# Attention over a patched on-chip pool: blocks kept in SBUF, 16 pairs instead of 32 sequences

## The reference

```
x = x + einsum('bct,bcd->bdt', x, W0[cond])                     # layer 0: a 32 x 32 mix per sequence
x = x + x @ W1.T + scaled low-rank adapter (rank 16 of 8)        # layer 1
q, k, v = x @ Wq.T, x @ Wk.T, x @ Wv.T                           # layer 2: 8 query heads, 4 key heads of 32
q, k = rope(rms(q)), rope(rms(k))                                # positions kv_lens .. kv_lens + 31
blk = block_tables[b, pos // 16]
k_blocks[blk, :, pos % 16] = k;  v_blocks[blk, :, pos % 16] = v  # the new rows are written into the pool first
scores = q . all keys of the sequence's table, masked to the last 128 positions; softmax; . v;  @ Wo.T
x = x + attention;   x = x + x @ W3[id] + b3[id]                 # layer 3: one of 16 experts per sequence
```

## Time and profile before

| | |
|---|---|
| runs | 164.04, 165.34, 165.74 us |
| profiled execution, first to last instruction | 177.7 us |
| mean granted TensorE clock in it | 0.932 |
| PE / DVE / ACT / POOL busy | 136.0 / 98.0 / 95.6 / 82.3 us |
| first scores | 63.9 us |

### The profile page before, as it was taken

The page is one execution under the profiler, slowest core; times in us unless marked ns, Lnnn a source line. Parts: engine busy times, 40 slices in busy tenths (PEclk is TensorE's granted clock), DMA queues, the critical chain, the costliest instruction groups (busy, mean ns, idle before and its releaser), DMA issues.

```text
span 177.7 us, 4258 instructions
## 1 busy us (share of the span) xinstructions
PE 136.0 (77%) x1414; PEld 93.1 (52%) x1414; DVE 98.0 (55%) x376; ACT 95.6 (54%) x288; POOL 82.3 (46%) x121
## 2 busy tenths in 40 slices
PE   0022989999899368969669659769959979999972
PEld 0012975999698233434235335357636556757741
DVE  0878803798346202795659356326746477975120
ACT  0007479694455724844999705446565666771200
POOL 3477500078377772185543876415677531421000
PEclk9999999999999978988999985856996999999999
DMA  4975990823793377012197776362256463655650
GB/s 89 331 174 178 404 411 24 365 107 118 295 376 101 96 253 330 0 65 59 36 391 272 216 204 191 122 220 73 89 195 191 114 211 115 185 156 161 204 178 31
DMA packets 21727, 32.57 MB, mean 183 GB/s; under 512 B 5162, under 2 KB 18730, under 8 KB 20682
## 3 DMA queue, kind: packets, MB, share of 16 engines
q1 hardware_dynamic: 15536, 19.76, 33.3%
q0 software_dynamic: 2960, 11.67, 18.9%
q10 hardware_dynamic: 3210, 0.87, 2.2%
HBM read 23.91 MB, written 8.39 MB: 182 GB/s over the span
## 4 chain that ended last, share of the span: by engine, by line
PE 67%; ACT 11%; issue 8%; DVE 6%; DMA 5%; another core or an unknown queue 2%; ACTq 0%; DVEq 0%
PE bank L1178 7%; PE bank L1162 7%; PE bank L1208 6%; PE bank L1221 5%; PE bank L1195 4%; PE bank L1066 4%; PE bank L1079 4%; PE bank L1055 4%; DMA kvn<-in_L_cond_weights,cond_i 3%; ACT pr L703 3%; PE bank L1216 3%; PE bank L1004 3%; ACT blkp L587 2%; PE bank L1039 2%; PE bank L1067 2%
## 5 line engine op out<-in xcount | busy, mean ns | idle before, releaser
L703 ACT ACTIVATE pr<-S,nb 128x160 f32<-128x160 f32 x64 | 27.0, 427 | 12.8 <-DVE nb L943 7.4
L943 DVE CUSTOM_DVE_ANT_0 S<-bank,mask 128x160 f32<-128x160 f32 x64 | 18.2, 319 | 17.5 <-PE bank L1162 10.2
L1162 PE MATMUL bank<-KT,QT 32*64 32x160 f32 x256 | 20.9, 341 | 6.2 <-DVE nb L943 3.4
L511 POOL TENSOR_TENSOR prB<-pr,ri 128x64 f32<-128x64 f32 x32 | 9.4, 295 | 29.8 <-DVE ri L928 29.7
L932 DVE TENSOR_SCALAR pr<-pr,ri 128x128 f32<-128x128 f32 x64 | 22.1, 389 | 1.1
L482 POOL DMA_INDIRECT blkp<-kv_rows,rowA x16 | 16.9, 1058 | 7.7 <-DMA kv_rows<-blkp 5.4
L482 POOL DMA_INDIRECT kvA<-kv_rows,rowA x16 | 16.3, 1022 | 6.4 <-issue 3.4
L690 ACT COPY PTA<-bank 128x256 f32<-128x256 f32 x32 | 12.0, 375 | 13.0 <-PE bank L1178 10.2
L1162 PEld LDWEIGHTS bank<-KT,QT 32*64 32x64 f32 x256 | 8.8, 138 | 15.9 <-issue 9.6
L1178 PE MATMUL bank<-cst,pr 128*128 128x128 f32 x64 | 14.0, 304 | 0.5
L703 ACT ACTIVATION_READ_ACCUMULATOR pr<-S,nb 128x1 f32 x64 | 12.5, 195 | 0.0
(11 more groups left out here) (206 smaller groups left out, 313.1 us busy)
## 6 DMA issues: line engine op xcount, KB each, us to landing
We<-in_L_cond_W SPq DMA_DIRECT2D x16, 256.0 KB
kvn<-in_L_cond_W SPq DMA_DIRECT2D x16, 256.0 KB
kv_rows<-blkp SPq DMA_DIRECT2D x1, 2048.0 KB, 6.5
kv_rows<-blk SPq DMA_DIRECT2D x1, 2048.0 KB
kv_rows<-blkp SPq DMA_DIRECT2D x4, 512.0 KB, 4.9
xin<-in_x SPq DMA_DIRECT2D x2, 512.0 KB, 5.6
kv_rows<-kvn SPq DMA_DIRECT2D x2, 512.0 KB, 2.8
be<-in_L_cond_b SPq DMA_DIRECT2D x32, 32.0 KB
```

Of the source, the lines that this page charges most:

```text
L703: act.activation(pr[:, n // B4 % 2, u, n % B4, :], S[:, n % 2, u, :], ACT.Exp, bias=nb[:, n % 4, u:u + 1], scale=-1.0, accum_out=rs[:, n % ...
L943: dve.tensor_tensor_reduce(S[:, n % 2, u, :], bank[2 + (2 * n + u) % 3][:, 0:KEYS], mask[:, n, :], -SCALE, 3e38, ALU.add, ALU.min, nb[:, n ...
L1162: i_ = mm(bank[2 + i % 3][GS * T * k:GS * T * k + GS * T, 0:KEYS], QT[h, g, j, :], KT[h, g % 2, j, :], start=True, stop=True)
```

## The change

Nearly every function is touched. What it does:

- **Blocks.** A unit now holds the 11 blocks of 11, 11 and 10 sequences. All eight raw transfers (the 96 blocks that are written, K and V, and three units of K and V) are of 128 blocks; POOL issues them in one run. The permuted units stay in SBUF (`blkp`), by row in the block.
- **Writes.** The 96 written blocks go to DRAM (`wr_rows`, 1.5 MB), eight indexed stores put the 1,024 new rows there, and three indexed loads copy the finished written blocks over those partitions of `blkp` whose block was written; other indices are out of bounds and skipped. The 40 gathers of rows are gone.
- **Keys** are turned on PE from `blkp` (`turn_k`, 12 calls of 4, L1043), into KT for all 32 sequences. **Values** go out with the unit to DRAM (2 MB, `values_out`) and come back by row (`values_back`, four transfers of 512-byte pieces a unit).
- **Masks.** One strip of 318 distances is squared and compared once, written to DRAM, and read back 32 times at 32 offsets (`load_mask`, 128 pieces of 352 bytes). The 32 distance rows on ACT and the 8 mask instructions on DVE are gone.
- **q** is projected from x2 after layer 1, two products a tile, with no composed Wq; layer 1 and all q norms now come before the loop.
- **Loop** of 16 pairs over 176 columns (before 160): one exponential per sequence and half as before, but one normalising per pair on POOL (L520, 128 x 704), one copy of 512 and one of 256 columns on ACT. On PE the product with V trails the scores by three pairs, before by eight sequences. Tails are turned per pair.
- **Experts** are loaded without the biases (those are eight indexed loads on POOL); DVE adds the identity to each expert's diagonal blocks (L951), which replaces L1216. Sixteen experts have room where units 0 and 2 lay.
- **Start.** PE begins with 12 products of ones whose results nobody reads; W1 is loaded from ACT's queue, most small loads from SP's.

The core of the diff (removed lines are the old functions above; a line of "..." leaves lines out):

```
-            for n in range(B + TAIL):
-                if n + 1 < B:
-                    scores(n + 1)
...
+            for n in range(PAIRS):
+                if n + 1 < PAIRS:
+                    scores(n + 1)
+                for c in KT_STEP.get(n, ()):
+                    turn_k(c)
+                g = group_at(n, PROJECT)
+                if g is not None:
+                    project(g)
+                if n >= TURN:
+                    turn_probs(n - TURN)
+                if n >= PV:
+                    pv(n - PV)
+                if g is not None:
+                    layer3(g)
...
+            def load_mask(b):
+                x = sp.value_load(shift_i[0:1, b:b + 1], min_val=0, max_val=LAST)
+                sp.dma_start(mask[:, b, :], mask_rows[:, bass.ds(x, KEYS)]).then_inc(s_mask, 16)
...
+            for b in range(8):
+                load_mask(b)
+            for kv in range(2):
+                sp.wait_ge(s_perm[NU, kv], 1)
+            sp.dma_start(wr_blocks, blkw[0:NWI, :]).then_inc(s_base, 16)
+            for b in range(8, B):
+                load_mask(b)
...
+            values_out(0)
+            values_back(0)
+            values_out(1)
+            for b in range(4):
+                expert(b)
+            values_back(1)
+            values_out(2)
+            for b in range(4, 8):
+                expert(b)
+            values_back(2)
...
+            pool.wait_ge(s_new, 16 * NT)
+            pool.wait_ge(s_pidx, 1)
+            for u in range(NU):
+                for kv in range(2):
+                    pool.wait_ge(s_perm[u, kv], 1)
+                pool.indirect_dma_start(out=blkp[u][:, :], out_offset=None, in_=wr_blocks,
+                                        in_offset=bass.IndirectOffsetOnAxis(ap=patch_i[:, u:u + 1], axis=0),
+                                        bounds_check=NWI - 1, oob_is_err=False).then_inc(s_patch[u], 16)
...
+            for p in range(PAIRS - 1):
+                pool.wait_ge(s_ri, p + 1)
+                e_ = pr[:, p % 2, :, :].rearrange("p u r -> p (u r)").rearrange("p (i r) -> p i r", i=4)
+                pool.tensor_tensor(e_, e_, ri[:, p % 2, :].unsqueeze(2).broadcast_to([P, 4, KEYS]),
+                                   ALU.mult).then_inc(s_pn, 1)
...
+                    if n == 0:
+                        dve.wait_ge(s_mask, 16 * B)
+                        dve.wait_ge(s_new, 16 * NT)
...
+                    dve.wait_ge(s_we[g % B4], 16 * B4 * (g // B4 + 1))
+                    for kc in range(KC):
+                        w_ = We4(g)[:, :, kc, kc * P:(kc + 1) * P]
+                        tt(w_, w_, ident.unsqueeze(1).broadcast_to([P, B4, P]), ALU.add).then_inc(s_wx, 1)
```

More of the change, by code:

```diff
@@ L380, in _ @@
             for g in range(NT):
[L381 removed]
+                while nxt < B and (nxt - NE) // B4 <= g - 1:
                     expert(nxt)
@@ L544, in distances @@
-            def distances(g):
-                for j in range(B4):
-                    distance(g, j)
+            act.wait_ge(s_kvT, 1)
+            act.copy(WkvT, square(0)).then_inc(s_kvTk, 1)
+            act.wait_ge(s_mixz, 1)
+            act.wait_ge(s_mixt, 1)
+            for h, q in MIX_ACT:
+                dst, src = mix_part(h, q)
+                act.copy(dst, src).then_inc(s_mixA, 1)
+            act.wait_ge(s_w1T, 1)
+            act.copy(W1T, square(0)).then_inc(s_w1Tk, 1)
+            act.wait_ge(s_aT, 1)
@@ L1058, in project_kv @@
-            def project_kv(v, i):
-                pe.wait_ge(s_xas, i + 1)
+            def project_kv(v, i, tiles=(0, 1, 2, 3)):
+                if not v and tiles[0] == 0:
+                    pe.wait_ge(s_xas, i + 1)
+                    pe.wait_ge(s_cmpk, 2)
+                    pe.wait_ge(s_aTk, 2)
                 w = slice(KV * v, KV * v + KV)
-                for t in range(4):
+                for t in tiles:
                     o = bank[1 + 2 * v + i][:, t * KV:t * KV + KV]
@@ new lines, in _ @@
+            mix_down(0)
+            mix_down(1)
+            pe.wait_ge(s_qw, 16)
+            turn_square(7, nat, 1).then_inc(s_qT, 1)
+            pe.wait_ge(s_diag, 4)
+            pe.wait_ge(s_set, 2)
+            pe.wait_ge(s_w1Tk, 1)
+            for u in range(4):
+                n = PU[u] if u < NU else NWI
+                c0 = UCOL[u] if u < NU else FLAT
+                i_ = mm(bank[0][0:NWI, c0:c0 + n], ones[0:n, 0:NWI], diag[0:n, u, 0:n], start=True, stop=True)
+            i_.then_inc(s_brd, 1)
@@ new lines, in _ @@
+            CNT = FLAT + NWI
+            down(0)
+            pe.wait_ge(s_inr, 3)
+            mm(bank[0][0:NWI, CNT:CNT + BLOCK + 1], later[:, :], wr[:, 2, :], start=True, stop=True).then_inc(s_cnt, 1)
+            down(1)
+            pe.wait_ge(s_can, 1)
+            mm(bank[0][0:NWI, CNT + 20:CNT + 21], same[:, :], own[:, 0:1], start=True, stop=True)
+            for u in range(NU):
+                i_ = mm(bank[0][0:PU[u], CNT + 24 + u:CNT + 25 + u], hit[:, UCOL[u]:UCOL[u] + PU[u]], own[:, 0:1], start=True, stop=True)
```

1425 lines of the change are left out of this document (671 added, 754 removed).

## The result

| | before | changed |
|---|---|---|
| runs, median (us) | 165.34 | 154.90 (154.64 to 156.95) |
| profiled execution, span (us) | 177.7 | 153.1 |
| spans of single runs (us) | | 152.9, 153.1, 155.1 |
| mean granted clock | 0.932 | 0.90 |
| PE / DVE / ACT / POOL busy (us) | 136.0 / 98.0 / 95.6 / 82.3 | 117.3 / 88.8 / 85.8 / 62.0 |

The changed kernel takes 0.952 of the time before, 95% interval 0.938 to 0.967. It is faster, by 10 us and not by 24. The forecast of the span, 152, is met within 1.1 us, and every run of the changed kernel is 1.8 us above its own span. The forecast of the run time, 141, is missed by 14.

The account below looks back on a forecast made before the run. PE was taken to bound the loop. First scores at 71, 63.3 of PE's loop, 10 of fill, drain and bubbles, 3.0 of output, 3 for clock, 2 overlooked gave a span of 152 us; as runs 141, range 130 to 157.

Parts of the forecast that it names:

- As runs: Last step: span 152 converted to run time by the old profile's 12.4 us excess, as constant or ratio, giving 141.
- Up to the first scores: Stage before the loop: first scores at 71 us, 7 us later than in the kernel before.
- The covers: POOL's stores, patches and bias gathers, mask loads and values, each costed at nothing as hidden under other work.
- Mask loads: Loads on SP's queue, 1.15 us each, the last 24 ending at 59 us; costed at nothing.
- rival 3: Masks late: DVE's first maximum waits for all 32 loads; at 2.9 us a load, runs 169; chance 0.08.
- Values: Trip through DRAM: a 2 MB unit lands 6.5 us after issue, out at 60, back by 73; costed at nothing.
- The loop's groups: PE's group of four sequences in the loop: 7.33 us against 8.24, eight groups 58.6.
- The remaining allowances: Added to PE's loop work: 10 us for fill, drain and bubbles, 3 for the clock, 2 for what is overlooked.
- A rule against the change: In the loop, DVE's identity additions with two SBUF inputs and POOL's normalising shut each other out for their whole length.
- rival 2: POOL and DVE shut each other out in the loop: 11 us more, span 163, runs 151.5; chance 0.07.
- Rival 1: Lost clock and waits return in the loop, values late through one SP queue: span about 165, runs 153; chance 0.19.

Follow-up runs that it names:

- before_again: The kernel before, unchanged, profiled once more: 163.79 us, span 161.8.
- unit2_after_base: Changed kernel, with POOL asking for the third raw unit's blocks only after the written blocks have landed: 152.42 us.
- one_mask: Changed kernel with 31 of the 32 mask loads left out, every sequence using the first mask: 149.17 us.
- masks_later: Changed kernel with masks 8 to 15 loaded after the written blocks' landing, 16 to 31 behind the first values' issue: 164.15 us.
- no_value_trip: Changed kernel without values going to DRAM and back, SP issuing eight experts from the loop's start: 136.28 us.
- pv_interleaved: Changed kernel with main and tail by turns in the product with V, as before the change: 156.34 us.
- identity_on_pe: Changed kernel with the identity added by products on PE in layer 3 instead of DVE's additions: 155.05 us.
- after_again: The changed kernel, unchanged, measured again on one chip with the kernel before: 156.03 us, ratio 0.899.
- masks_after_base: Changed kernel, only V written out, third unit read after written blocks land, 20 mask loads behind that landing, 4 behind first values: 151.98 us.

## Why the prediction was wrong in the time, and what of it was right

**The step that failed is the last one, "As runs".** The sum, 152, was built upwards from PE's products, DVE's norms and issues; nothing in it was a difference from 177.7. It then needed only what lies between a span and its own run, 1.6 to 1.8 us in every run of both kernels here. I took off 10.6 to 12.4 us instead, because the profile of before was 12.4 above the median. The two readings I offered, a constant and a ratio, both carry a property of one execution of the old kernel over to the new one. before_again shows what it was: an execution longer than those that were timed, by "remote" waits and a lower clock between 90 and 140 us; what caused them stays open. 152 + 1.8 = 153.8 would have stood against 154.9, a gain of 7% on the median of 165.34 and not of 15%. One reading of the sum hangs on the same execution: its lost clock, 12 us from 60 to 140, is 80 x 0.06 = 4.8 us in before_again (clock 0.94 there). The group of 8.24 us is the same in both.

**That the span was met is partly two errors that cancel.** Point by point:

- *Up to the first scores.* Forecast 71; DVE's first maximum starts at 74.53 us, released by PE's scores and by no DMA. The last root is at 64.09 (forecast 65), so the norms were right. Behind it ACT waits for turned keys, and PE for patches, which I had costed at nothing. ACT's timeline and then PE's (start, length, what, idle before and its releaser) show the chain of it:

```profile
67.05 0.56 ACT L610 COPY kt_m<-bank 128x484 f32<-128x484 f32 x1 [1.14 <-PE bank L1043]
...
71.77 1.03 ACT L610 COPY kt_m<-bank 128x484 f32<-128x484 f32 x2 [1.28 <-PE bank L1043]
```

```profile
65.87 3.47 PE L1043 MATMUL bank<-cst,blkp 121*128 121x121 f32 x16 [6.13 <-DMA blkp<-wr_rows,patch_i]
...
71.10 1.05 PE L1043 MATMUL bank<-cst,blkp 121*128 121x121 f32 x8 [1.32 <-DMA blkp<-wr_rows,patch_i]
...
73.49 0.83 PE L1063 MATMUL bank<-kt_m,natQ 32*64 32x176 f32 x16 [0.91 <-ACT natQ L598]
```

  From the last root to the first scores, at 73.49, it is 9.4 us and not 6. Of the 3.4 us more, ACT's waits for turned keys are 3.1 (the two shown and three of 0.2).
- *The covers.* The written blocks were to go out at 31 and land well before the stores at 43; they went out at 28.50 and landed at 44.96. That is the first size that was off: I had put no length on it. POOL waited 19.1 us for them, its eight stores end at 56.80 instead of 48, and the patches are issued at 59.09 to 63.31 instead of by 54. The third raw unit makes some 4.2 us of the 16.5 (unit2_after_base), the masks as a whole 4.6 (one_mask), but not the 24 loads beside it (masks_later).
- *Mask loads.* Issue at 1.15 us each was near: one follows another by 1.13 us in the first eight and by 1.33 in the 24 from 29.65 to 60.6 us. They were not late, so rival 3 fell. They cost 5.7 us by another way, through the written blocks, which went out 2.7 us later for them and landed 4.6 us more slowly.
- *Values.* Out at 60, landed at 66, back at 73 was the forecast; out at 65.89, landed at 78.93, then a second unit that takes 10.34. The 6.5 us of the earlier trace rows came from engines with a share of 0.76 (31 to 37.5 us of before); from 81 to 91.4 us here the profile gives a share of 1.07 at 358 GB/s. Here is the term that was mis-sized most: 13.0 and 10.3 for 6.5, each with the return behind it and the experts behind that. I had it at nothing, under a cover; no_value_trip prices the whole trip at 18.6 us.
- *The loop's groups.* Forecast 7.33, measured 6.15 us. The identity and key turnings went nearly as counted (0.64, 0.59 and 0.26 in the old group, for 0.64, 0.59 and 0.15). Of the rest, the scores of four sequences fell from 1.72 to 1.52 us though they grew by a tenth, with 16 products in a row where there were 8; products with V went from 4 x 0.38 to 4 x 0.29, layer 3 from 1.02 to 0.90; and the turnings cost 1.47 against 1.40 where I had added 0.3. Eight groups make 9.4 us less than I forecast. That longer rows of like products are what makes them cheaper is argued; no run isolates it, and the order within the products with V is excluded by pv_interleaved.
- *The remaining allowances* (fill, bubbles, 3 for the clock, 2 for what is overlooked, together some 15) were spent by the transfers. So that the span was met is luck: the groups came out 9.4 us too dear and the allowances too large, against transfers costed at nothing. Without the value trip the span is 134.4: 152 − 9.4 = 142.6, and some 8 of the 15 not needed.
- *A rule against the change.* L520 takes 1.45 us in the mean (forecast 1.43): 1.36 in most cases and 1.72 where an addition had started just before it. Two additions on DVE take 1.29 us alone and 2.43 beside such a one. Alone, then both engines of one meeting:

```profile
107.10 1.29 DVE L951 TENSOR_TENSOR blkp<-blkp,cst 128x512 f32<-128x512 f32 x2 [6.71 <-DMA blkp<-in_L_cond_W]
```

```profile
119.78 2.43 DVE L951 TENSOR_TENSOR blkp<-blkp,cst 128x512 f32<-128x512 f32 x2
```

```profile
119.94 1.72 POOL L520 TENSOR_TENSOR xin_m<-xin_m,ri 128x704 f32<-128x704 f32 x1 [1.12 <-DVE ri L924]
```

  The Trainium skill (SBUF — State Buffer, SBUF: two separate sides) says that a DVE instruction with two SBUF inputs and a POOL instruction that reads SBUF shut each other out for their whole length. By that rule, the trace agrees: POOL gets longer while the first addition runs, and the second then ends 0.55 us behind POOL. In four groups DVE loses 1.1 us so; identity_on_pe, without the additions, is no faster. The watch I set, "L951 well over 0.7 speaks for rival 2", was no good test: it showed the collision, not a price.
- *Rival 1* had the right mechanism: clock at 0.78 in the middle, and values and experts as releasers, all through SP's queue. It got 0.19. Its price of 165 on the span's scale kept the slow groups that did not come; that its run time of 153 lies near 154.9 is luck, by the same wrong 12 us. Rival 1's own text held the point that should have moved the chances: three streams through one queue, against covers that were each costed with empty engines.

**What stays open.** Why the first transfer of values takes 13 to 14 us with one MB or two, with the engines 38% busy in its last 3 us; what the kernel before waits for in its long executions; why the written blocks land sooner with fewer masks ahead of them; whether the experts, placed elsewhere, need not wait for the values' landing; and whether the experts' loads could come through another queue, which was not tried.

## What to carry to other kernels

A sum built from the bottom stands on its own: convert it to run time by what lies between a span and its own run, and do not carry what a long execution of the old kernel has over to the new one. When several covers are costed at nothing, give each transfer a length, write down which one must have landed before the next is issued, and add up that chain; add their bytes per stretch too, and compare with the rate that the engines reached when full. Each transfer here was given its cover, the chain of them had none. A transfer's length read from a row holds for the load on the engines in that row, and here it was exceeded even where they were not full to the end.

## What the runs showed of the hardware that was not expected

- Full DMA engines moved 300 to 360 GB/s in these windows (share 0.91 at 303, 0.97 at 362); a transfer of 2 MB that took 6.5 us at a share of 0.76 took 10.3 in full engines, and 13.0 to 14.3 in a place where they emptied before it landed; one of 1.5 MB took 9.7 to 17.8 us over all the runs.
- 31 mask loads of 128 pieces of 352 bytes, 1.4 MB in all, cost 5.7 us of the kernel's time. Leaving them out shortened the landing of a neighbour by 4.6 us, moving the 24 beside it away did not (15.8 us in masks_later against 15.1 in after_again).
- SP issued such a load, with its register load, every 1.1 to 1.3 us; sixteen in a row occupied it for 20.5 us (masks_later), four behind a transfer in 512-byte pieces for 12.6 (masks_after_base).
- DVE additions with two SBUF inputs, two of them, took 1.29 us alone and 2.43 beside a POOL multiplication of 704 columns, which took 1.72 us in place of 1.36.
- One kernel differs by 10 to 12 us between chips, and another, with the same inputs and outputs, by 1, so a ratio between two kernels is a property of the chip as well.
- 16 products of 64 x 176 in a row took 0.76 us, two runs of 8 of 64 x 160 took 0.86.
